# Causal attention with the scores kept: a new order at the turns of query blocks, and every copy of scores out of PSUM on ScalarE

## The reference, cut to what matters

```python
q, k, v = x @ Wq + bq, x @ Wk + bk, x @ Wv + bv          # 4096 x 128 each, one head
scores = q @ k.T / sqrt(128), causal                     # 4096 x 4096, lower triangle
out = softmax(scores) @ v @ Wo + bo
x = layernorm(x + out)
```

## Time and profile before

| | |
|---|---|
| median of 3 runs | 1553.49 us (1553.38 to 1556.54) |
| the profiled execution | 1558.12 us, its span 1556.4 us |
| busy over the span | PE 94%, PEld 68%, DVE 62%, ACT 50%, POOL 21% |
| stage C, by its r, sub and exp jobs | about 1010 to 1395 us of the span |
| mean granted clock of TensorE | 0.964 of full speed |

### The profile page before, as it was taken

The page is one execution under the profiler, slowest core; times in us unless marked ns, Lnnn a source line. Parts: engine busy times, 40 slices in busy tenths (PEclk is TensorE's granted clock), DMA queues, the critical chain, the costliest instruction groups (busy, mean ns, idle before and its releaser), DMA issues. The chain is left out here.

```text
span 1556.4 us, 24716 instructions
## 1 busy us (share of the span) xinstructions
PE 1456.5 (94%) x10064; PEld 1062.3 (68%) x10064; DVE 964.7 (62%) x1840; ACT 779.8 (50%) x1099; POOL 327.6 (21%) x198
## 2 busy tenths in 40 slices
PE   8999999999999998999999999978877898889998
PEld 6677777777777775445455555556766687787886
DVE  3355546464635477977877877843666565566665
ACT  4333333333333335886787788734455554542333
POOL 0021112121111132000000000014457456720001
PEclk9999999999999999999999999989888899999999
DMA  7203131203031160010110010015000000021112
GB/s 263 79 27 107 30 104 54 101 33 106 32 102 46 43 209 28 1 55 1 55 55 28 28 55 1 0 41 148 27 28 28 27 1 1 1 85 52 54 55 81
DMA packets 48131, 88.38 MB, mean 57 GB/s; under 512 B 7201, under 2 KB 15009, under 8 KB 46610
## 3 DMA queue, kind: packets, MB, share of 16 engines
q1 hardware_dynamic: 48018, 86.80, 16.5%
HBM read 57.43 MB, written 29.36 MB: 56 GB/s over the span
## 5 line engine op out<-in xcount | busy, mean ns | idle before, releaser
L1004 PE MATMUL psum<-early,high 128*128 128x512 fp8e4 x1024 | 235.7, 382 | 6.9 <-DVE low_r L976 4.2
L1004 PEld LDWEIGHTS psum<-early,high 128*128 128x128 fp8e4 x1024 | 98.9, 99 | 127.5 <-issue 7.8
L411 POOL TENSOR_TENSOR rms<-ms,mhalf 128x16 f32<-128x16 f32 x30 | 87.8, 2926 | 343.1 <-DVE ms L474 343.1
L126 PE MATMUL psum<-Qh_r,Kh 128*128 128x512 f32 (+1 forms) x272 | 113.9, 419 | 14.6 <-DVE c_gm L1459 14.3
L1459 DVE TENSOR_TENSOR c_gm<-psum,c_gm 128x512 f32<-128x512 f32 (+2 forms) x136 | 87.3, 642 | 61.6 <-ACT c_rows L1383 32.2
L1011 PE MATMUL psum<-high,b_act 128*128 128x512 fp8e4 x512 | 115.4, 379 | 1.0 <-DVE Ql_r L981 0.8
L126 PE MATMUL psum<-early_r,high_r 128*128 128x512 f32 x256 | 107.0, 418 | 5.5 <-DVE early_r L437 5.5
L128 PE MATMUL psum<-Qh_r,Kl 128*128 128x512 f32 (+1 forms) x272 | 107.0, 393 | 0.0
L127 PE MATMUL psum<-Ql_r,Kh 128*128 128x512 f32 (+1 forms) x272 | 106.5, 392 | 0.0
L128 PE MATMUL psum<-early_r,low_r 128*128 128x512 f32 x256 | 101.9, 398 | 0.0
L127 PE MATMUL psum<-early_r,high_r 128*128 128x512 f32 x256 | 101.3, 396 | 0.0
(11 more groups left out here) (273 smaller groups left out, 3472.2 us busy)
## 6 DMA issues: line engine op xcount, KB each, us to landing
low<-x_dram SPq DMA_DIRECT2D x9, 1024.0 KB, 5.6
wst<-in_L_ffn_w_gating SPq DMA_DIRECT2D x16, 512.0 KB, 4.5
xs<-in_L_attn_x SPq DMA_DIRECT2D x8, 1024.0 KB, 7.6
high<-x_dram SPq DMA_DIRECT2D x8, 1024.0 KB, 8.1
xt<-in_x_turned SPq DMA_DIRECT2D x7, 1024.0 KB, 4.8
x_dram<-xs SPq DMA_DIRECT2D x7, 1024.0 KB, 4.9
x_dram<-low SPq DMA_DIRECT2D x5, 1024.0 KB, 4.3
wst<-in_L_ffn_w_linear SPq DMA_DIRECT2D x16, 256.0 KB, 4.4
```

The source lines that it names most:

```text
L126: tensor.matmul(out, hi_w, hi_x, start=first, stop=False, skip_group_check=True)
L411: nc.gpsimd.tensor_tensor(rms_of(b, c), ms_of(b, c), const["mhalf"][:, 0:H], ALU.pow).then_inc(*done)
L1004: last = t.matmul(out[:, h, :], w8g[:, tile + k, (2 * m + h) * P:(2 * m + h + 1) * P], x8[:, u, k, :], start=k == 0, stop=k == DC - 1)
```

## The change

Parts of it, in the order of the diff:

1. `units`: tiles 0 and 1 of each block from 1 on are single units.
2. `points`: for blocks below 6 the raw scores of the next block are wanted two tiles earlier.
3. A marker job `exps` stands behind the last pv of the block before and ahead of the next r jobs. The exps are appended there and at each pv (`raise_up`), no longer at mb.
4. oT and y of the block before are put beside units 1, 3, 4, ... in place of 0, 2, 3, ...; by tiles, y stands where it stood.
5. `on_dve` is empty: all 144 copies are ACT's. The copy waits for the maximum, and the bank comes free with the copy.
6. `bo(i)` goes into POOL's list right behind the last sub of its block i, for i up to 6.
7. `nb` is split: `neg` on DVE (minus the mean, 128x4) and the multiplication with rstd on POOL.
8. The plan: at the start, the exps of block 0 move behind a stretch of stage B, with stage B's V^T job of block 6 ahead of pv(0,0). At the end, x(0,0) to x(0,3) of stage D move from behind pv(7,6), pv(7,8), pv(7,10), pv(7,12) to behind mb(7), pv(6,26), pv(7,0) and pv(7,1).

```diff
+        return [(k, 1) for k in (0, 1) if i] + [(k, 2) for k in range(2, CH * i, 2)] + [(k, 1) for k in range(CH * i, tiles(i))]
+    def alone(i, k):
+        return k < 2 or k >= CH * i
...
-    points = [(4, 16), (9, 24)] + [(2 * (i + 1) * (i + 2) - 8, ...
+    points = [(4, 16), (9, 24)] + [(2 * (i + 1) * (i + 2) - (10 if i < NB - 2 else 8), ...
...
         outputs = [("oT", i - 1)] + [("y", i - 1, c) for c in range(CH)]
+        order.append(("exps", i))
...
-            if outputs and (u != 1 or i == 1):
+            if outputs and (u not in (0, 2) or i == 1):
...
-    on_dve = {x[1:] for n, x in enumerate(raws) if n % 4 == 3}
+    on_dve = set()
...
+            if x[1] == tiles(x[0]) - 1 and x[0] < NB - 1:
+                pool_order.append(("bo", x[0]))
+    def raise_up(i, k):
         while to_exp and to_exp[0] <= (i, k + 5):
             act_order.append(("exp", *to_exp.pop(0)))
...
+        elif kind == "exps":
+            raise_up(i, -2)
         elif kind == "pv":
             soften(i, name[2])
+            raise_up(i, name[2])
...
-                later = [([], []), ([("nb", i)], [])] + ...
-                pool_order.append(("rstd", i))
+                dve_order += [("var", i), ("neg", i)]
+                later = [([], []), ([], [])] + ...
+                pool_order += [("rstd", i), ("nb", i)]
...
-            uses[name] = (V, ("max", *name[1:]))
+            uses[name] = copied(*name[1:])
...
-        opening = {("pv", last, 6 + 2 * k): ("x", 0, k) for k in range(DC)}
+        opening = dict(zip((("mb", last), ("pv", last - 1, CH * last - 2), ("pv", last, 0), ("pv", last, 1)), [("x", 0, k) for k in range(DC)]))
```

More of the change, by code:

```diff
@@ L1075, in stage_c @@
     rl = s.sb("c_rl", [P, CH], F32)
+    neg = s.sb("c_neg", [P, CH], F32)
     w_in = s.sem("c_w_in")
@@ L1162, in stage_c @@
             emit_raws(2)
+        if k == 0:
+            order.append(("exps", 0))
         emit_pv(0, k, 1)
@@ L1211, in soften @@
             (dve_order if x in subs_on_dve else pool_order).append(("sub", *x))
+            if x[1] == tiles(x[0]) - 1 and x[0] < NB - 1:
+                pool_order.append(("bo", x[0]))
+    def raise_up(i, k):
         while to_exp and to_exp[0] <= (i, k + 5):
             act_order.append(("exp", *to_exp.pop(0)))
-    for n, name in enumerate(order):
+    pe_order = []
+    for name in order:
         kind, i = name[0], name[1]
+        if kind != "exps":
+            pe_order.append(name)
         if kind == "r":
+            dve_order.append(("max", *name[1:]))
             (dve_order if name[1:] in on_dve else act_order).append(("cp", *name[1:]))
-            dve_order.append(("max", *name[1:]))
             if name[1:] == (1, CH):
@@ L1249, in stage_c @@
             if c == CH - 1:
-                dve_order.append(("var", i))
-                later = [([], []), ([("nb", i)], [])] + [([], [("norm", i, c), ("norm", i, c + 1)]) for c in (0, 2)]
-                pool_order.append(("rstd", i))
+                dve_order += [("var", i), ("neg", i)]
+                later = [([], []), ([], [])] + [([], [("norm", i, c), ("norm", i, c + 1)]) for c in (0, 2)]
+                pool_order += [("rstd", i), ("nb", i)]
         if later and (kind == "pv" or i == NB - 1 and kind in ("oT", "y")):
@@ L1256, in stage_c @@
             act_order += act_steps
-        counts.append((name, (n + 1, len(act_order), len(dve_order), len(pool_order))))
+        counts.append((name, (len(pe_order), len(act_order), len(dve_order), len(pool_order))))
     dve_order += [x for steps, _ in later for x in steps]
     act_order += [x for _, steps in later for x in steps]
-    counts[-1] = (name, (len(order), len(act_order), len(dve_order), len(pool_order)))
+    counts[-1] = (name, (len(pe_order), len(act_order), len(dve_order), len(pool_order)))
     V = Steps(s.sem("c_dve"), dve_order, 0)
@@ L1273, in stage_c @@
     n_r = n_m = 0
-    for name in order:
+    for name in pe_order:
         kind, i = name[0], name[1]
@@ L1355, in pool_engine @@
                 k = name[2]
-                wait_for(pool, 0, (A, ("mb", i)), copied(i, k), copied(i, k + (k < CH * i)))
-                if k < CH * i:
+                wait_for(pool, 0, (A, ("mb", i)), copied(i, k), copied(i, k + (not alone(i, k))))
+                if not alone(i, k):
                     both = home_of(place[i, k // 2])
@@ L1371, in pool_engine @@
                 nc.gpsimd.tensor_tensor(xs[i], xs[i], bo[:, None, :].broadcast_to([P, CH, D]), ALU.add).then_inc(*L.done(*name))
+            elif kind == "nb":
+                wait_for(pool, 0, (V, ("neg", i)), (L, ("rstd", i)), *([(A, ("norm", i - 1, CH - 1))] if i else []))
+                nc.gpsimd.tensor_tensor(nb[:, :], neg[:, :], rstd[:, :], ALU.mult).then_inc(*L.done(*name))
             else:
@@ L1452, in vector_engine @@
                     needs.append((prev["M"], ("y", NB - 2, CH - 1)))
-                if (i, k) not in on_dve:
-                    needs.append((A, ("cp", i, k)))
                 wait_for(dve, 0, *needs)
@@ L1486, in vector_engine @@
             else:
-                wait_for(dve, 0, (L, ("rstd", i)), *([(A, ("norm", i - 1, CH - 1))] if i else []))
-                nc.vector.scalar_tensor_tensor(nb[:, :], mv[:, :, 0], -1.0, rstd[:, :], ALU.mult, ALU.mult).then_inc(*done)
+                wait_for(dve, 0, (V, ("ba", i, CH - 1)), *([(L, ("nb", i - 1))] if i else []))
+                nc.vector.tensor_scalar(neg[:, :], mv[:, :, 0], -1.0, None, ALU.mult).then_inc(*done)
     def tensor_engine(pe, names):
@@ L1535, in tensor_engine @@
             last.then_inc(*M.done(*name))
-    return dict(order=order, pe=order, act=act_order, dve=dve_order, pool=pool_order, cuts=cuts_of(counts), banks=banks, uses=uses, free=free,
+    return dict(order=order, pe=pe_order, act=act_order, dve=dve_order, pool=pool_order, cuts=cuts_of(counts), banks=banks, uses=uses, free=free,
                 M=M, A=A, V=V, L=L, spill=spill, gpsimd=pool_engine, vector=vector_engine, scalar=scalar_engine, tensor=tensor_engine,
```

21 lines of the change are left out of this document (9 added, 12 removed).

## The result

The changed kernel takes 1551.07 us (median of 20 runs, 1548.37 to 1552.58) against 1555.26 us (1552.90 to 1558.71) for the kernel before: a ratio of 0.9972, 95% interval 0.9966 to 0.9978. By the ratio it is 4.4 us faster, where 29 were forecast; the time lies outside the range of 1510 to 1547. The profiled execution has a span of 1549.0 us at a mean clock of 0.974, against 1556.4 at 0.964.

A forecast was written before the change was run, and what follows sets the result against it. PE bounds the kernel, idle mainly at block turns and then at half clock. Turns 16.5, start 4.4, last block 9.0, DVE 2.6, less 0.5 and 3.0, give 29.0 us: 1524.5 from 1553.5, range 1510 to 1547.

The forecast's parts named there:

- The failed step: Turn into block 6: pv(6,2) starts 7.4 us behind mb's copy, not 12.45; gain 5.0, or 4.5 after one copy.
- turns, with DVE's 2.6 and ACT's -3.0: Turns into blocks 1 to 6 gain 16.5 us; DVE's shorter waits add 2.6, ACT's extra copies cost 3.0.
- start: Start of stage C: copies no longer behind block 0's exps save 3.2 us of PE wait; with clock, 4.4.
- last block, with the tail's -0.5: Block 7 into stage D: turn 2.5, h(0) and x jobs make 10.7, taken as 9.0; norm(7)'s wait for nb costs 0.5.
- copies on ACT alone: 36 score copies moved from DVE to ACT: ACT longer than PE per unit where norms run, 3.0 us lost.
- The first product: pv(i,0) at each turn starts earlier with the single unit: into block 6, 2.1 us behind mb's copy, 4.5 earlier.
- Into block 4: Norms ahead of the exps, pv(4,0) at about 1184.4 against 1188.74; gain taken as 5.0 us.
- Into 5: PE waits 4.58 us for an r job's bank, its copy behind the first pair's exp; gain 0.
- Rival A: Waits move: ACT's copies behind exp(i,2) bound all turns as r jobs spill ahead of pv(i,0); 1541 us, chance 0.17.
- B: Slower: ACT becomes the bound between the turns, its copies holding up exps; 1559 us, chance 0.11.
- nb: The layer norm's 128x4 product on POOL takes 0.5 us, hidden except at the end.
- neg: 128x4 on DVE takes 0.17 us, or up to 1.2 if a port rule holds; hidden seven of eight times.

The follow-up runs named there:

- e3_pairs: The changed kernel with tiles 0 and 1 made one pair unit again: 1523.28 us, ratio 0.9783 to the kernel before.
- m1_norms: The changed kernel with shorter exp reach at single units, block 1's oT(0) and y(0,0) one unit later, norm steps not advanced at pv(i,1): 1525.03 us.
- e4_x_late: The changed kernel with stage D's four x jobs put back behind pv(7,6) to pv(7,12): 1555.64 us, ratio 0.9998 to the kernel before.
- f1_one_ahead: The changed kernel with tiles 0 and 1 paired again and exp reach one unit shorter at the marker and pv(i,0): 1525.49 us, ratio 0.9798.
- l2_plans_back: The changed kernel with tiles 0 and 1 paired, every fourth copy on DVE and both plans as before, block 0's marker kept: 1528.51 us, ratio 0.9816.
- g1_marker: The kernel before with only the marker `exps` added for blocks 1 to 7: 1544.14 us, ratio 0.9942.
- h1_copies_alone: The kernel before with only `on_dve` emptied, so all 144 copies run on ACT: 1553.35 us, ratio 0.9991.
- the best version: Changed kernel: pairs in blocks 1 to 5, singles in 6 and 7, shorter exp reach, every fourth copy on DVE, points at 8 tiles: 1513.41 us.

## Why the prediction was wrong

**The failed step** is in the turn into block 6, and in its use for the other turns: the working ends at the start of pv(i,2), "7.4, where pv(6,2) starts", and takes the 5.0 us gained there as the gain of the turn. Up to that point it was nearly right. Read off the timelines, in us behind the end of mb's copy:

| block | 1 | 2 | 3 | 4 | 5 | 6 | 7 |
|---|---|---|---|---|---|---|---|
| pv(i,0), before | 3.7 | 5.5 | 3.7 | 9.0 | 9.2 | 6.7 | 6.3 |
| pv(i,0), changed | 2.2 | 2.2 | 2.2 | 4.0 | 9.2 | 2.2 | 3.2 |
| pv(i,0), e3_pairs | 3.7 | 3.7 | 3.7 | 4.4 | 10.4 | 3.7 | 4.7 |
| pv(i,2), before | 9.2 | 11.6 | 9.4 | 15.5 | 14.1 | 12.8 | 10.6 |
| pv(i,2), changed | 12.7 | 7.3 | 8.0 | 16.3 | 14.1 | 7.7 | 6.4 |

In block 6 pv(6,0) comes at the forecast 2.1 and pv(6,2) at 7.7, 5.0 earlier than before. (mb's copy itself comes 1.1 us later behind mb(6) than before, where 0.5 were taken for the copy ahead of it.) What stands in ACT's list behind exp(6,2) and the next two copies was not counted:

```profile
1296.84 1.06 ACT L1426 ACTIVATE Ql<-Ql 128x1024 f32<-128x1024 f32 x1 [1.68 <-POOL Ql L1375]
1297.81 1.07 ACT L1402 ACTIVATE high<-psum 128x512 f32<-128x512 f32 x2
1299.18 1.06 ACT L1426 ACTIVATE high<-high 128x1024 f32<-128x1024 f32 x1 [0.30 <-POOL high L1375]
1301.50 1.06 ACT L1426 ACTIVATE high<-high 128x1024 f32<-128x1024 f32 x1 [1.27 <-POOL high L1375]
1302.47 0.58 ACT L1408 ACTIVATE c_oh<-psum 128x512 fp32r<-128x512 f32 x1
...
1305.11 0.50 PE L126 MATMUL psum<-Qh_r,Kh 128*128 128x512 f32 x1 [2.80 <-ACT Qh L1402]
```

Before, exp(6,6) stood behind `oh` and the next copy. Now it stands ahead of them, and the second r job behind pv(6,2) waits 2.80 us. The exps that the marker puts into ACT's list were counted; those that pv(i,0) and pv(i,1) add were not. The reach is 5 tiles, and it is measured from each pv: with a pair, exp(i,6) comes at pv(i,2), behind oT and the next copies; with two single units it comes at pv(i,1), ahead of them. The layer norm's steps are counted per pv as well, and so are the outputs in block 1. All three put work ahead of the copies, and a bank that now comes free with the copy passes it on to PE. Measured one after the other by the ratios: reach 0.0098 (15 us), block 1's outputs, with what they move in block 2, 0.0036 (6 us), norms 0.0037 (6 us). That is 27 of the 29 us between the changed kernel and e3_pairs (0.0189). The first two are beyond their intervals; the third rests on the waits named above as well.

The single units also moved r jobs on PE: between oT(3) and pv(4,2) stand six of them and not the two of the kernel before and of e3_pairs, and pv(4,2) starts 0.8 us later than before. No experiment takes this alone; m1_norms still has it and is level with the paired kernels.

By the prediction's terms:

| term | forecast, us | measured |
|---|---|---|
| turns, with DVE's 2.6 and ACT's -3.0 | 16.1 | -10.3 from mb(1) to mb(7); +14.7 in m1_norms (248.8 against 263.5) |
| start | 4.4 | 3.5 from mb(0) to mb(1); 5.0 in e4_x_late, whose lists are the same up to there |
| last block, with the tail's -0.5 | 8.5 | 10.3 from mb(7) to the end |
| ahead of mb(0) | 0 | 3.9, at most 1.3 of it the change's |
| copies on ACT alone | -3.0 | -5 in the changed order, 0 with pairs, 0 to +1 alone |

- **The first product** did come forward. Against e3_pairs in the table the single unit has 1.5 us of this in blocks 1, 2, 3, 6 and 7, but only 0.4 in block 4; the rest comes with a pair too. Into block 4, from mb(4) to pv(4,0), the kernel before takes 10.1 us (1178.61 to 1188.74), the changed one 5.3 (1187.05 to 1192.32): 4.8, where the prediction took 5.0. In e3_pairs it is 5.7. But mb(4) itself came 8.4 us late, and three r jobs later PE stood still once more:

```profile
1192.32 3.21 PE L1541 MATMUL psum<-V,Qh 128*128 128x129 f32 x16 [2.75 <-ACT Qh L1429]
...
1201.58 0.50 PE L126 MATMUL psum<-Qh_r,Kh 128*128 128x512 f32 x1 [3.09 <-ACT Qh L1402]
```

- **Into 5** nothing was forecast, and PE's wait grew from 4.58 to 5.75 us. e3_pairs has 5.62 there, so this one is not the single unit's; f1_one_ahead has 3.32. The stretch from mb(5) to mb(6) is 4.5 us shorter all the same. l2_plans_back has this too (51.9 us) and g1_marker not (57.2), so it comes from nb, bo, points or banks.
- **Rival A** named the mechanism, ACT's copies as the bound at the turns, but for r jobs that spill ahead of pv(i,0), and priced it at 1541. It held that gains go to nothing; in the turns into 1, 2 and 3 they turned to losses. B's mechanism, an ACT that is full in the dense stretches, did not show: h1_copies_alone is no slower than before.
- **The last block.** `oh` behind exp(7,6) was seen by the prediction there, and only there. PE does not wait at h(0), and its matmuls run at full clock, 0.39 to 0.47 us a row:

```profile
1368.01 1.95 PE L1541 MATMUL psum<-V,high 128*128 128x129 f32 x16
...
1369.72 0.47 PE L126 MATMUL psum<-Kh,early_r 128*118 128x512 f32 x1
```

  The x jobs hold 4 to 5 us of the 10.3 (e4_x_late), not the 8.2 of the sum, and the turn the rest, where 2.5 were forecast. The 9.0 came out near the 10.3 by luck: two errors cancel.
- **The start.** PE waits 2.1 us in place of 5.2, 3.1 less where 3.2 was forecast; l2_plans_back shows that it comes from block 0's marker.
- **nb** on POOL takes 0.20 us where 0.5 was taken, and no 128x4 operation of DVE lasts over 1.2 us; `neg` takes 0.17 in all eight cases:

```profile
L1390 POOL TENSOR_TENSOR c_nb<-c_neg,c_rstd 128x4 f32<-128x4 f32 x8 | 1.6, 198 | 1.1
...
L1505 DVE TENSOR_SCALAR c_neg<-c_mv 128x4 f32<-128x4 f32 x8 | 1.4, 170 | 0.0
```

  The Trainium skill (SBUF — State Buffer, Who interferes with whom) had given reason to fear up to 1.2 us for it. The prediction had neg start when rstd does. In all eight cases of the changed kernel neg ends before rstd begins (in the last block 1368.56 and 0.17 us long, rstd at 1368.73), and rstd begins 0.25 us after the start of var, as before. The two never overlap, so these rows do not test the rule for `tensor_scalar`. What the earlier trace rows show for one nb holds for more: of the eight in the kernel before, six lie beside a POOL operation, three times bo and three times a sub, and end at most 0.03 us after it; the other two take 0.15 and 0.16 us.

What stays open: how the 16 to 20 us between g1_marker and l2_plans_back divide. By place the traces have 4.3 us from mb(0) to mb(1), 5.3 from mb(5) to mb(6) and 3.2 behind mb(7). Block 0's marker is the larger part of the first; for nb, bo, points and banks only single removals were tried, each with 3 us or less, and of the cover that one gives the other only nb and bo were seen.

## What to carry to other kernels

When a list is filled "so many units ahead at each unit", halving a unit changes what stands ahead of what on every engine whose list hangs on that loop. Write out each engine's list around the edited place before and after, over the next few jobs and not only up to the first that the edit is for, and count what is ahead of the instruction that frees a buffer. And price a split past the job that it is for: here the first two products came as worked out, and the stop followed behind them. The same edit lost 28 us over seven turns; in the last two blocks, with the exps held as they were, it gave 2.4 us at most, by one pair of traces.

## What the runs showed that was not expected

- A DVE operation of 128x4 with two inputs in SBUF took 1747 ns in the mean with bo (128x2048) issued at gT and 883 ns with bo at the end of its block; `neg`, the same size with one input, took 170 ns.
- 36 copies of scores on ACT in place of DVE cost 5 us in one order of ACT's list and nothing measurable in two others, at the same 0.59 us each.
- In the best version the granted clock averages 0.986 over the span, against 0.964 before, with PE's busy time 1433.7 us against 1456.5 for the same 10064 matmul instructions: 23 of its 45 us of span are matmuls that take less time. 19 of the 23 lie behind mb(0), where fewer run at the lower level behind a stop: from mb(0) to mb(7) the clock is 0.96 against 0.89.
